# A per-token scan on one core: the product with q moved from GpSimd to VectorE for half of the heads

## The reference, cut to what matters

```python
def step(S, inp):
    qt, kt, vt, at, bt = inp
    Sd = at[..., None, None] * S
    u = vt - jnp.einsum('bhk,bhkv->bhv', kt, Sd)
    Sn = Sd + bt[..., None, None] * kt[..., None] * u[:, :, None, :]
    o = jnp.einsum('bhk,bhkv->bhv', qt, Sn)
    return (Sn, o)
```

## Time and profile before

| | |
|---|---|
| median of 3 runs | 2117.53 us (2116.58 to 2126.91) |
| the profiled execution, its own time | 2123.31 us |
| its span, first to last instruction | 2121.6 us |
| busy in the span: PE, DVE, ACT, POOL | 81%, 64%, 55%, 13% |
| mean granted TensorE clock | 0.913 |
| the scan, from the first ka to the last add | 39.4 to 187.4 us |

### The profile page before, as it was taken

The page is one execution under the profiler, slowest core; times in us unless marked ns, Lnnn a source line. Parts: engine busy times, 40 slices in busy tenths (PEclk is TensorE's granted clock), DMA queues, the critical chain, the costliest instruction groups (busy, mean ns, idle before and its releaser), DMA issues.

```text
span 2121.6 us, 27925 instructions
## 1 busy us (share of the span) xinstructions
PE 1719.7 (81%) x10314; PEld 784.9 (37%) x10314; DVE 1361.8 (64%) x2651; ACT 1161.4 (55%) x2115; POOL 273.5 (13%) x352
## 2 busy tenths in 40 slices
PE   5797074379999999999857975989889998499998
PEld 3797072012222222222223432444444443334443
DVE  6988865689999999999423345555666655322222
ACT  5564003058888888888961336655666655222222
POOL 4453003000000000000010001111111111111110
PEclk9999586579999999999987987999999999599999
DMA  1000001510000000000102420000000000112421
GB/s 41 1 1 1 0 1 52 81 17 2 2 2 2 2 2 2 2 2 2 32 11 52 91 46 1 16 5 12 15 16 15 16 0 1 37 42 43 60 54 26
DMA packets 76525, 42.57 MB, mean 20 GB/s; under 512 B 21968, under 2 KB 72272, under 8 KB 76400
## 3 DMA queue, kind: packets, MB, share of 16 engines
q1 hardware_dynamic: 75008, 37.90, 8.7%
q10 hardware_dynamic: 1392, 3.02, 0.7%
HBM read 37.55 MB, written 3.15 MB: 19 GB/s over the span
## 4 chain that ended last, share of the span: by engine, by line
PE 51%; DVE 31%; ACT 8%; DMA 5%; issue 3%; POOL 1%; SPq 0%; ACTq 0%; DVEq 0%; POOLq 0%
DVE MX L944 17%; PE PS L1426 6%; PE PS L999 5%; PE PS L1432 5%; PE PS L1858 4%; PE PS L1859 4%; PE PS L1868 4%; PE PS L1021 3%; DMA SB<-scr_w 3%; ACT tmpb L1065 3%; PE PS L1377 3%; PE PS L512 2%; PE PS L1396 2%; PE PS L1268 2%; DVE MS L613 2%
## 5 line engine op out<-in xcount | busy, mean ns | idle before, releaser
L1065 ACT ACTIVATE tmpb<-PS 128x512 f32<-128x512 f32 x1024 | 554.0, 595 | 145.3 <-PE PS L1021 128.8
L944 DVE TENSOR_REDUCE MX<-PS 128x2 f32<-128x1024 f32 x512 | 585.2, 1216 | 56.6 <-PE PS L926 52.6
L999 PE MATMUL PS<-tmpb,VS 128*32 128x256 f32 x4096 | 325.1, 392 | 14.1 <-ACT tmpb L1065 6.6
L926 PE MATMUL PS<-KST,QST 56*128 56x512 bf16 x1024 | 206.7, 401 | 64.7 <-DMA KST<-scr_k 37.0
L1021 PE MATMUL PS<-QST,KST 59*128 59x512 bf16 x1024 | 200.7, 389 | 22.0 <-ACT tmpb L1065 16.1
L1893 DVE TENSOR_TENSOR HG<-HG,PS 128x512 f32<-128x512 f32 (+1 forms) x96 | 65.9, 686 | 199.3 <-PE PS L1859 199.3
L1883 ACT ACTIVATE HG<-PS 128x512 f32<-128x512 f32 (+1 forms) x96 | 57.2, 596 | 207.8 <-PE PS L1858 207.8
L999 PEld LDWEIGHTS PS<-tmpb,VS 128*32 128x32 f32 x4096 | 82.4, 108 | 177.4 <-issue 82.7
L1021 PEld LDWEIGHTS PS<-QST,KST 59*128 59x128 bf16 x1024 | 49.1, 93 | 243.8 <-ACT tmpb L1065 227.2
L1426 PE MATMUL PS<-X,WF 128*128 128x512 f32 x256 | 128.5, 637 | 4.2 <-ACT X L1571 4.2
L1587 ACT ACTIVATE HF<-PS,CL 128x512 f32<-128x512 f32 x128 | 88.0, 687 | 68.7 <-PE PS L1426 68.7
(11 more groups left out here) (295 smaller groups left out, 2508.0 us busy)
## 6 DMA issues: line engine op xcount, KB each, us to landing
SB<-scr_w SPq DMA_DIRECT2D x16, 1024.0 KB, 14.5
WF<-in_L_attn_Wf SPq DMA_DIRECT2D x16, 256.0 KB, 3.0
QST<-NMP SPq DMA_DIRECT2D x192, 1.0 KB
G<-in_L_ffn_w SPq DMA_DIRECT2D x16, 176.0 KB, 2.3
QST<-scr_q SPq DMA_DIRECT2D x14, 192.0 KB
W<-in_L_ffn_w SPq DMA_DIRECT2D x16, 128.0 KB, 2.2
scr_q<-tmpb SPq DMA_DIRECT2D x3, 512.0 KB, 2.7
KST<-scr_k ACTq DMA_DIRECT2D x14, 96.0 KB
```

The source lines that it names most:

```text
L926: pe.matmul(PS[:, b + x, :], QST[r, 2 * g + jj, CH * qc + P * t:CH * qc + P * t + P], KST[r, g, cs(kc)], start=True, stop=True).then_inc(s ...
L944: r = v.tensor_reduce(MX[:, :, m // (TPC * NC), m // NC % TPC, m % NC], PS[:, b:b + 2, :], AX.X, ALU.max)
L999: last = pe.matmul(PS[32 * j:32 * j + 32, 3, h], VS[:, kt, u // NC, :], PB[:, kt % 2, j, h], start=(kt == 0 and half == 0), stop=(kt == NT ...
L1065: a.activation(PB[:, kt % 2, j, :], PS[:, at % 3, :], ACT.Exp, scale=HD ** -0.5).then_inc(s_exp, 1)
```

## The change

GpSimd computes the product with q only for half 1. For half 0 it is now VectorE's, issued at the end of each token, behind add 1. The one semaphore of the products becomes two, one for each half, and whoever waited for the shared count now waits for the count of its half or of both. The semaphore `s_asig`, for which nothing waited, goes.

```diff
+        s_qsx, s_red, s_ov = [sem(f"s_qs{x}") for x in range(2)], sem("s_red"), sem("s_ov")
...
             for s in tokens:
                 a.wait_ge(s_amm, s + 1)
-                a.activation(SG[:, s, :], PS[:, s % 4, 0:NQ], ACT.Sigmoid).then_inc(s_asig, 1)
+                a.activation(SG[:, s, :], PS[:, s % 4, 0:NQ], ACT.Sigmoid)
...
                 if s + 1 < NT:
                     v_ka(v, s + 1, 0)
                 v_add(v, s, 1)
+                qs(v, s, 0)
...
             if s >= 2:
-                v.wait_ge(s_qs, hx(s - 2, x))
+                v.wait_ge(s_qsx[x], s - 1)
...
-        def g_qs(g, s, x):
-            g.wait_ge(s_state, hx(s + 1, x))
+        def qs(e, s, x):
+            e.wait_ge(s_state, hx(s + 1, x))
             if s >= 1:
-                g.wait_ge(s_red, hx(s - 1, x))
+                e.wait_ge(s_red, hx(s - 1, x))
...
-            g.tensor_tensor(QS[:, :, heads(x), :], hb(QK[:, s, 0:D], x), SS[(s + 1) % 2][:, :, heads(x), :],
-                            ALU.mult).then_inc(s_qs, 1)
+            e.tensor_tensor(QS[:, :, heads(x), :], hb(QK[:, s, 0:D], x), SS[(s + 1) % 2][:, :, heads(x), :],
+                            ALU.mult).then_inc(s_qsx[x], 1)
...
         def g_a0(g, chain):
             for s in range(NT):
-                for x in range(2):
-                    g_qs(g, s, x)
+                qs(g, s, 1)
...
         def pe_o(pe, s, x):
-            pe.wait_ge(s_qs, hx(s, x))
+            pe.wait_ge(s_qsx[x], s + 1)
...
         def act_spread(a, k):
             a.wait_ge(s_rt, k + 1)
-            a.wait_ge(s_qs, hx(NT - 2, 1))
+            for x in range(2):
+                a.wait_ge(s_qsx[x], NT - 1)
...
         def v_chain(v, chain):
-            v.wait_ge(s_qs, hx(NT - 1, 1))
+            for x in range(2):
+                v.wait_ge(s_qsx[x], NT)
```

More of the change, by code:

```diff
@@ L222, in build @@
         S0t = sb("S0t", [P, HD, H0, HD], F32, a0)
-        s_amm, s_asig, s_av, s_aev = sem("s_amm"), sem("s_asig"), sem("s_av"), sem("s_aev")
+        s_amm, s_av, s_aev = sem("s_amm"), sem("s_av"), sem("s_aev")
         s_kn2, s_ksq = sem("s_kn2"), sem("s_ksq")
         s_state, s_as, s_pr, s_w, s_kw = sem("s_state"), sem("s_as"), sem("s_pr"), sem("s_w"), sem("s_kw")
-        s_qs, s_red, s_ov = sem("s_qs"), sem("s_red"), sem("s_ov")
+        s_qsx, s_red, s_ov = [sem(f"s_qs{x}") for x in range(2)], sem("s_red"), sem("s_ov")
         s_rt, s_rv, s_ra = sem("s_rt"), sem("s_rv"), sem("s_ra")
@@ L465, in v_add @@
                             ALU.add).then_inc(s_state, 1)
-        def g_qs(g, s, x):
-            g.wait_ge(s_state, hx(s + 1, x))
+        def qs(e, s, x):
+            e.wait_ge(s_state, hx(s + 1, x))
             if s >= 1:
-                g.wait_ge(s_red, hx(s - 1, x))
+                e.wait_ge(s_red, hx(s - 1, x))
             if s == NT - 1:
                 q = hb(QK[:, s, 0:D], x)[:, :, :, 0:HD]
-                g.tensor_tensor(QS[:, :, heads(x), 0:HD], q, SF[:, :, 0, heads(x), :], ALU.mult)
-                g.tensor_tensor(QS[:, :, heads(x), HD:SCOL], q, SF[:, :, 1, heads(x), :], ALU.mult).then_inc(s_qs, 1)
+                e.tensor_tensor(QS[:, :, heads(x), 0:HD], q, SF[:, :, 0, heads(x), :], ALU.mult)
+                e.tensor_tensor(QS[:, :, heads(x), HD:SCOL], q, SF[:, :, 1, heads(x), :], ALU.mult).then_inc(s_qsx[x], 1)
                 return
-            g.tensor_tensor(QS[:, :, heads(x), :], hb(QK[:, s, 0:D], x), SS[(s + 1) % 2][:, :, heads(x), :],
-                            ALU.mult).then_inc(s_qs, 1)
+            e.tensor_tensor(QS[:, :, heads(x), :], hb(QK[:, s, 0:D], x), SS[(s + 1) % 2][:, :, heads(x), :],
+                            ALU.mult).then_inc(s_qsx[x], 1)
         def act_state(a):
```

## The result

The changed kernel takes 2140.33 us in the median of 6 runs (2137.62 to 2147.53), the kernel before 2117.06 in the median of 6. The profiled execution took 2139.17 us with a span of 2137.3, 15.7 above that of before. One execution out of ten of the kernel with both products on VectorE, further down, took 7927 us where the others took 2123 to 2142; it counts as slow and is not in that kernel's ratio.

The account below looks back on a forecast made before the run. The scan's token loop through TensorE and VectorE, 8.54 us a token, was taken as the bound. Terms -0.76 + 0 + 15.1 + 1.19 = +15.5 us on the 2117.5 median gave 2133.0 us, range 2115 to 2141.

Parts of the forecast that it names:

- GpSimd is served: Likeliest case, chance 0.62: in steady tokens GpSimd's product runs before ka 1, which starts 1.82 us late; +15.5 us in all.
- token 0: First token of the scan: its ka 0 is no longer held by GpSimd's half 0 product, -0.76 us.
- tokens 1 to 3: Early scan tokens: the added VectorE product costs 1.14 us, saved before L413 and in ka 0; 11.36 against 11.34, nothing.
- 11 steady tokens: Tokens 4 to 14 of the scan: each grows from 8.54 to 9.91 us, +1.37 a token, +15.1 us.
- token 15: Last token, from add 1 of token 14 to the last add: ka 1 held up, +1.19 us.
- Who gets the port at 1.00: Behind add 1, as VectorE's q product ends: GpSimd let in at 1.00, before ka 1's record could start at 1.06.
- VectorE keeps the port: Rival, chance 0.28: ka 1 runs before GpSimd's product; steady token 8.69 us, +0.9 us in all, 2118.4, not slower.
- The price of the product on VectorE: The full-size q product (128x1024) moved to VectorE takes 1.22 us, as ka, the same instruction in form.
- Nobody waits in `s_red`: VectorE's q product at the end of each steady token starts 0.08 us before add 1 ends, its awaited sum long done.
- the clock falls: Rival, chance 0.03: TensorE, busy 79% of a steady token, gets a lower clock; +37 us in all, 2154.
- Behind the scan: After the last add, both products of the last token end 3.6 us later instead of 2.39; VectorE's 3.38 us idle covers it.
- The upper bound of a gain: Most that any split of the products could give: 11 x 0.68 + 0.76 = 8.3 us, 0.4%.

Follow-up runs that it names:

- the second set: The changed kernel run once more, unedited, against the kernel before: ratio 1.0079 (1.0054 to 1.0103), steady token 9.90 us.
- the earlier product: The changed kernel with VectorE's product with q issued behind add 0 instead of add 1: ratio 1.0037 to the kernel before, steady token 8.89 us.
- the fill: The changed kernel with GpSimd filling half 1 with zeros instead of multiplying: ratio 0.999 to the kernel before, steady token 8.73 us.
- the half length: The changed kernel with GpSimd's product done for 4 of its 8 heads, except in the last token: ratio 0.9997 to the kernel before.
- the token of 8.23: Against the kernel before: a quarter of the product on VectorE, TensorE reordered, half 0 of QS double-buffered; ratio 0.9993, steady token 8.23 us.

## Why the prediction was right, point by point

The forecast was 2133.0 us (2115 to 2141), slower with a chance of 0.62, by the case that GpSimd is served. The median is 2140.33, inside the range but only 0.7 below its upper end. The span was to be 2137.1 and is 2137.3, but that agreement is in part luck: the scan grew by 1.3 us more than forecast, and the rest of the span shrank by 1.1.

| term | predicted (us) | measured (us) |
|---|---|---|
| token 0 | -0.76 | -0.91 (12.21 to 11.30) |
| tokens 1 to 3 | 0 | +1.49 (34.01 to 35.50) |
| 11 steady tokens | +15.1 | +14.97 (93.98 to 108.95) |
| token 15 | +1.19 | +1.21 (7.81 to 9.02) |
| last add to the joining of the pieces | 0 | 0 (15.26 in both) |
| the rest of the span | 0 | -1.1 |

The rest is what is left when the span's +15.7 loses the scan's +16.8; it consists of a scan that starts 0.54 earlier and later stages that scatter. The sum in microseconds fits the two profiles. By the ratios on record the change costs 20 us (15 to 25), in the second set 17 (11 to 22); the bare medians are 23.3 and 15.4 us apart. The forecast of 15.5 lies at the lower edge of the first and inside the second. What the first set has above 15.5 no trace shows. The base scatters as much: over the sets the kernel before has medians of 2117.06, 2121.02 and 2124.12, where I had taken 2117.5.

*Who gets the port at 1.00* was the one open step, and it fell to GpSimd in all 11 steady tokens, with ka 1 at 3.05 where I had written "about 3.0". I argued from 0.06 us between the end of the hold and the start of the next record. The outcome fits that (the hold ended 1.00 behind add 1, ka 1's record started 1.05 behind it), but no run varied this margin, so that it decides is not shown. What is shown, by the product in two instructions too (ka 1 at 2.12), is that in these contests the side that waited went next at each end of an instruction. That VectorE keeps the port is refuted, by 11 steady tokens of 11 in each of the two profiles.

*The price of the product on VectorE* (1.22) was right: 1.218, from ka, the same form on the same tiles.

*Nobody waits in `s_red`*: right, VectorE's product starts 0.08 or 0.09 before add 1 ends in each steady token.

*Tokens 1 to 3* were right in two of three (11.36 for 11.36). Token 3 failed, by the rival "the clock falls", which I had given 0.03 for the steady tokens and argued against with the 1.00 of tokens 1 to 3 before. It fell in one token, and in the second profile a little in token 1 as well, where it cost nothing; token 3 was lengthened by 1.4 and 0.8 us in the two profiles. What draws it is open: the kernel with both products on VectorE and the one with GpSimd's in two have it in token 3 as well (a clock of 0.86 in both, 12.40 and 12.27), those with the earlier product, the fill and the half length don't (1.00; 11.68, 10.11, 10.44), but have a clock of 0.79, 0.90 and 0.91 in token 1. No run here isolates it.

*Behind the scan* the cover held; of the 3.38 us of slack 0.89 were used. The step to the joining was 3.29 and not 3.6: I had VectorE do both of its halves first and GpSimd then both of its own, while the port passed from one to the other behind each half.

*The upper bound of a gain* (0.4%) is 11 x 0.68 + 0.76 = 8.2 us, not 8.3, and leaves tokens 1 to 3 out without a reason. No version came near it: the token of 8.23 shows that some of it can be had, but what that gives, 0.2% of this kernel's time, is within what one run differs from the next.

## What to carry to other kernels

In these runs GpSimd's fp32 product and VectorE's fp32 products and sums with two SBUF operands ran one after the other where they met, but for the last 0.13 to 0.14 us of a record (GpSimd's at 3.06 and 2.94 for 2.02, add 0 at 1.79 and ka 1 at 3.05 for 1.22). So moving the product from one to the other freed nothing by itself. What counted was which VectorE instruction came next when GpSimd got the port: kw 0, with an operand in PSUM, stayed at 1.22 under GpSimd's product, and with it in that place the token was 8.89 us instead of 9.90. In a kernel like this one, put such an instruction where a GpSimd product gets the port, and keep GpSimd's instructions short, since ka 1 behind them paid nearly their whole length (1.83 us of 2.02, 0.90 of 1.10). Find such waits by comparing records of the same form, and not in the chain of waits, which here called ka 1's wait of 1.80 us issue. The gain was small, since the products were off the chain to begin with: no version was clearly faster than the kernel before.

## What the runs showed of the hardware that was not expected

- The port passed at the end of an instruction to the side that waited, in either direction: to GpSimd in between two VectorE products (all 11 steady tokens of the changed kernel, where the record of VectorE's next starts only 0.05 us behind the point of the change), and to VectorE in between two GpSimd products (ka 1 at 2.12 instead of 3.05, in two instructions). It was taken over 0.13 to 0.14 us before the record of the holder ends.
- A dip of TensorE's granted clock (0.86 from 73.61 to 85.68, 0.83 from 77.30 to 87.20 in the second profile; matmul groups of 2.05 us at 2.7 to 3.3) came in the same token, token 3, in both profiles of one kernel. In both, TensorE was busy 8.33 or 8.34 us of the 11.36 of the token before it, more than the 8.13 of 11.34 at which the kernel before kept 1.00. What draws it is open.
